# A decoder kernel's first attention stages: stack units and cross slots moved, batch 0's cross mask added in PSUM

## The reference

```python
x = x + _L0_attn_ref(_layernorm(x), Wq, Wk, Wv, Wo, lambda_q1, ...)      # differential, 8 heads x 2
x = x + _L0_xattn_ref(ctx, ctx, _layernorm(x), mask, W_fc, b_fc)          # 16 heads of 8

def _L0_xattn_ref(value, key, query, mask, W_fc, b_fc):
    energy = jnp.einsum('nqhd,nkhd->nhqk', q, k)
    energy = jnp.where(mask == 0, -1e20, energy)
    attention = jax.nn.softmax(energy / jnp.sqrt(E), axis=3)
    out = jnp.einsum('nhql,nlhd->nqhd', attention, v).reshape(N, Sq, E)
    return out @ W_fc.T + b_fc
```

## Time and profile before

| what | us |
|---|---|
| median of 3 runs | 1274.69 |
| lowest, highest | 1274.1, 1276.63 |
| profiled execution | 1273.83 |
| its span | 1272.5 |
| PE, DVE, ACT, POOL busy | 1040.1, 812.6, 610.1, 232.6 |

### The profile page before, as it was taken

The page is one execution under the profiler, slowest core; times in us unless marked ns, Lnnn a source line. Parts: engine busy times, 40 slices in busy tenths (PEclk is TensorE's granted clock), DMA queues, the critical chain, the costliest instruction groups (busy, mean ns, idle before and its releaser), DMA issues.

```text
span 1272.5 us, 19904 instructions
## 1 busy us (share of the span) xinstructions
PE 1040.1 (82%) x7649; PEld 557.8 (44%) x7649; DVE 812.6 (64%) x2015; ACT 610.1 (48%) x1015; POOL 232.6 (18%) x299
## 2 busy tenths in 40 slices
PE   6777689998999965677675889999647978769999
PEld 4233223333677652344542333566412333346757
DVE  7787867722115468878776881677688886565422
ACT  2456356564334428768652677323115556323342
POOL 2933300000000223765621000001210000010000
PEclk9789779997899985766876999999857888779999
DMA  8342140000000300346014202600100300000000
GB/s 299 91 87 67 41 160 2 2 2 1 1 1 1 100 34 1 105 122 125 1 44 136 100 2 35 106 1 1 50 23 11 119 1 2 33 1 1 1 9 9
DMA packets 34785, 61.29 MB, mean 48 GB/s; under 512 B 4771, under 2 KB 25076, under 8 KB 33092
## 3 DMA queue, kind: packets, MB, share of 16 engines
q1 hardware_dynamic: 33828, 58.70, 16.5%
q10 hardware_dynamic: 864, 1.33, 0.3%
HBM read 42.98 MB, written 16.65 MB: 47 GB/s over the span
## 4 chain that ended last, share of the span: by engine, by line
PE 59%; DVE 29%; ACT 4%; issue 4%; DMA 2%; POOL 1%; SPq 0%; DVEq 0%; ACTq 0%; POOLq 0%
PE ps_s L851 9%; PE ps_e L841 9%; PE ps_v L644 6%; DVE mx L1798 6%; PE ps_e L580 5%; PE ps_e L578 3%; PE ps_s L601 3%; PE ps_e L938 2%; PE ps_s L925 2%; DVE ps_s L1794 2%; DVE mx L1788 2%; DVE work L2274 2%; ACT work L1346 2%; DVE work L2276 2%; DVE xn L1754 1%
## 5 line engine op out<-in xcount | busy, mean ns | idle before, releaser
L1346 ACT ACTIVATE work<-ps_e 128x512 f32<-128x512 f32 x448 | 250.6, 598 | 149.4 <-PE ps_e L580 144.1
L2546 POOL TENSOR_TENSOR rstd<-rstd,halves 128x2 f32<-128x2 f32 x52 | 36.6, 704 | 752.8 <-DVE rstd L1741 752.7
L1798 DVE TENSOR_REDUCE mx<-ps_s 128x2 f32<-128x1024 f32 x128 | 153.9, 1222 | 28.8 <-PE ps_s L601 27.3
L601 PE MATMUL ps_s<-ctx_stack,q_stack 49*128 49x512 bf16 (+1 forms) x384 | 128.3, 452 | 50.0 <-DVE mx L1798 36.5
L1448 ACT ACTIVATE work<-ps_s,keep 128x512 f32<-128x512 f32 x136 | 93.0, 687 | 145.5 <-PE ps_s L851 142.5
L580 PE MATMUL ps_e<-q_stack,ctx_stack 52*128 52x256 bf16 (+1 forms) x768 | 150.9, 297 | 12.3 <-DMA q_stack<-mT 5.0
L644 PE MATMUL ps_v<-work,vaug 128*32 128x256 f32 x1536 | 133.2, 424 | 4.6 <-ACT work L1334 4.6
L841 PEld LDWEIGHTS ps_e<-ffn_w,work 128*128 128x128 f32 x960 | 119.3, 198 | 21.0 <-issue 19.9
L851 PE MATMUL ps_s<-xnT,ffn_w 128*128 128x512 f32 x240 | 119.7, 627 | 3.6 <-ACT work L1448 3.6
L841 PE MATMUL ps_e<-ffn_w,work 128*128 128x128 f32 x960 | 121.3, 282 | 0.8 <-DVE x L1990 0.8
L2000 DVE SCALAR_TENSOR_TENSOR x<-ps_e,gates,x 128x128 f32<-128x128 f32 x128 | 39.0, 347 | 127.0 <-PE ps_e L841 123.9
(11 more groups left out here) (373 smaller groups left out, 1812.1 us busy)
## 6 DMA issues: line engine op xcount, KB each, us to landing
q_stack<-q_scr SPq DMA_DIRECT2D x32, 192.0 KB
ffn_w<-in_L0f_w SPq DMA_DIRECT2D x1, 4608.0 KB, 14.7
ffn_w<-in_L1f_w SPq DMA_DIRECT2D x1, 3456.0 KB, 13.0
q_scr<-parts SPq DMA_DIRECT2D x16, 192.0 KB, 2.1
c_scr<-ffn_w SPq DMA_DIRECT2D x12, 256.0 KB, 7.6
kx_scr<-ffn_w SPq DMA_DIRECT2D x12, 256.0 KB, 3.5
ctx_stack<-kx_scr SPq DMA_DIRECT2D x2, 1536.0 KB
ctx_stack<-c_scr SPq DMA_DIRECT2D x2, 1536.0 KB
```

What stands on the lines that cost most here:

```text
L601: return pe.matmul(ps_s[i][:, parity, :], q_stack[p0:p0 + n_rows, b, pair, part * P:(part + 1) * P], ctx_stack[p0:p0 + n_rows, pair, b * S ...
L1346: act.activation(pt[:, parity, :, :].rearrange("p k q -> p (k q)"), bank[f"e{parity}"], ACT.Exp).then_inc(exped, 1)
L1798: m = dve.tensor_reduce(mx[:, b, :, pair, part], ps_s[i][:], AX, ALU.max, negate=True)
```

## The change

`OVERLAP` goes from 36 to 32. The queries' units of batch 1 leave the prologue for slots 0 to 3, its keys' units go from 0 to 3 to slots 4 to 7. The context units of batch 0 go from slots 3 to 10, one each, to slots 8 to 11, two each. Batch 0's x units go from 33, 34, 34, 35 to 30, 30, 31, 31; batch 1's from 41, 42, 42, 43 to 38, 38, 39, 39. The mask transposes go from 37, 38, 39, 45 to 33, 34, 36, 37. The norm for the cross stage is transposed and copied one slot earlier. In batch 0 each cross score bank is first filled with the mask by an identity matmul, and the score matmul adds to it; DVE then takes one plain negated reduction over both banks, and the sign change of L1807 is left out. PE waits for the two mask tiles of batch 0 before the first cross step. Batches 1 to 3 stay with the custom operation.

```diff
-OVERLAP = 36
+OVERLAP = 32
-STACK_FIRST = stack_units("q", 0), stack_units("k", 0) + stack_units("q", 1)
-MASK_AT = [37, 38, 39, 45]
+STACK_FIRST = stack_units("q", 0), stack_units("k", 0)
+MASK_AT = [33, 34, 36, 37]
 STACK_AT = {}
-for units, slots in ((stack_units("k", 1), range(4)), (stack_units("c", 0), range(3, 11)),
-                     (stack_units("x", 0), (33, 34, 34, 35)), (stack_units("x", 1), (41, 42, 42, 43)),
+for units, slots in ((stack_units("q", 1) + stack_units("k", 1), range(8)),
+                     (stack_units("c", 0), (8, 8, 9, 9, 10, 10, 11, 11)),
+                     (stack_units("x", 0), (30, 30, 31, 31)), (stack_units("x", 1), (38, 38, 39, 39)),
                      (stack_units("c", 1), (44, 44, 45, 45, 46, 46, 47, 47))):
...
             pair, part = h // 2 % 8, h % 2
+            masked = use == X0 and b == 0
+            if masked:
+                pe.matmul(ps_s[i][:, parity, :], ident_b[:], far_q[:, part, :], start=True, stop=False,
+                          skip_group_check=True)
             return pe.matmul(ps_s[i][:, parity, :], q_stack[p0:p0 + n_rows, b, pair, part * P:(part + 1) * P],
-                             ctx_stack[p0:p0 + n_rows, pair, b * S2:(b + 1) * S2], start=True, stop=True)
+                             ctx_stack[p0:p0 + n_rows, pair, b * S2:(b + 1) * S2], start=not masked, stop=True,
+                             skip_group_check=masked)
...
-                if at == 7:
+                if at == 6:
                     turn_norm("L0x", b)
...
+            if t == 0 and use == X0:
+                pe.wait_ge(far_done, TPB)
...
-                if at == 8:
+                if at == 7:
                     turned_norm("L0x", b, qT, scale=RSQRT128)
...
-                if use == X0:
+                if use == X0 and b > 0:
                     for parity in range(2):
                         m = dve.tensor_tensor_reduce(ps_s[i][:, parity, :], ps_s[i][:, parity, :],
...
-            if use == X0:
+            if use == X0 and b > 0:
                 settle(dve.tensor_scalar(col, col, -1.0, None, ALU.mult))
```

## The result

The changed kernel is slower by 0.7%: median 1281.55 us of 20 runs (1272.24 to 1293.13) against 1272.17 us of 20 runs of the kernel before (1263.6 to 1279.8). The ratio is 1.0072, 95% interval [1.0045, 1.0099], which is +9.2 us (5.7 to 12.6) where +11.2 was forecast. The profiled execution took 1276.23 us (span 1274.9), 5 us less than that median.

The account below looks back on a forecast made before the run. Latency before 172.2 us, then PE, bounds the kernel; only the shift of the first cross exponents counts. Terms -1.0 + 0 + 1.0 + 12.2 - 1.5 + 0.5 = +11.2 us, plus 0.86 on 1273.83: 1286 us, 8-in-10 range 1272.5 to 1292.

Parts of the forecast that it names:

- The tie: First cross exponents wait, through SP's fixed order, for batch 3's queries: 11.66 us after batch 3's norm transpose.
- E0: First exponent matmul of the cross stage, slot 56; at 162.21 us before, forecast at 173.4; its shift is the time change.
- Masks, +12.2: Batch 0's cross score steps: 13 masked steps on PE's path, each +0.94 us, together +12.2 us.
- lower end of 8.4: Mask term with no extra at the change from 128 rows to 56: a step grows by 0.65, 8.4 us.
- DVE, -1.5: Batch 0's cross maxima: plain reductions shorten DVE's work, counting only where PE waits for it; -1.5 us (0 to -2.9).
- Three more score steps, +1.0: Before batch 3's norm transpose: 19 score steps instead of 16, 0.33 us each, +1.0 us.
- units moved, 0: Batch 0's cross units, from slots 33 to 35 to 30 and 31, and batch 1's units: 0 (batch 0's ends -1, +1).
- Prologue, -1.0: Batch 1's query units leave the prologue, context units double up in slots 8 to 11: -1.0 us (-2.3 to 0).
- Split in slot 47, +0.5: DVE's split of batch 0's maxima falls between batch 3's close and its add: +0.5 us (0 to +2.5).
- After E0, unchanged: Stretch behind the first cross exponents keeps its length, 140 us to the mixture, with the same slots and closings left.
- Rival C: Slower: idle PE before E0 keeps the clock at 1.2 GHz longer, masked steps not hidden; +16.5 us, 1291, chance 0.11.
- Rival A: Faster: DVE and four earlier slots decide, PE's gaps take the masks whole; 5.2 us off, 1269.5, chance 0.14.

Follow-up runs that it names:

- moves only: The changed kernel without mask matmuls and the far_done wait, custom maximum for all batches, all slots moved; ratio 0.9983 to the kernel before.
- paired masks: The changed kernel with both mask matmuls ahead of both scores in each masked step; ratio 1.0024 to the kernel before.
- x4: The changed kernel with SP writing batch 0's maxima row ahead of batch 3's queries; ratio 1.0002 to the kernel before.
- x5: The changed kernel without mask matmuls, SP writing batch 0's maxima row ahead of batch 3's queries; ratio 0.9908 to the kernel before, median 1261.75 us.
- Masks only: The kernel before with batch 0's cross mask laid into PSUM by identity matmul and nothing moved; ratio 1.0032, median 1278.62 us.
- x11: The kernel before with batch 0's row placed after the write of batch 3's queries and ahead of their fill; ratio 0.9978, median 1269.54 us.
- x6: The kernel before with only SP's order changed, batch 0's row ahead of batch 3's queries; ratio 0.9962.
- x7: The kernel before with only the early query, key and context units moved as in the change; ratio 0.9988.
- x10: The kernel before with the early units moved and SP's order changed, cross slots still from 36; ratio 0.9968.
- x1: The kernel before with batch 0's cross mask laid into PSUM by identity matmul and nothing moved; ratio 1.0032.

## Why the prediction was right, point by point

The mechanism was right: the tie to batch 3's queries and the masks on PE's way. That the sum came so close (+11.2 for +9.2) is in part luck. Two terms that were put at nothing, the moved slots and the clock, were off by 3 to 4 us each, in opposite directions; the estimates stand in the last section.

**The tie.** "E0 is the transpose of batch 3's norm plus 11.66 us" held: 11.7 before, 12.0 in the changed kernel, 11.5 in moves only and 11.6 in paired masks, and 2.5 in x4 and x5, where SP's order was changed. This was the step on which the whole forecast rested, and x4 shows it.

**Masks, +12.2.** A step of mask, score, mask, score measured 1.28 us against 0.33: +0.95, forecast +0.94. The ratios put the masks with DVE's relief at 0.9% (changed against moves only) and 0.9% again (x4 against x5), some 11 to 12 us; the forecast had 12.2 - 1.5 = 10.7. Masks only (nine steps) came out lower, at 0.3%. The lower end of 8.4, a mask beside which nothing is lost at the change of row counts, is out: the score piece also took 0.32. The Trainium skill, page TensorEngine Tiling (Array Packing), section Key Properties under Tiling Modes, says that changing the tiling mode drains TensorE. It gives no size. The trace agrees with it: a step with two changes (paired) takes 0.86 us, one with four 1.28, some 0.2 us for each change that goes. But the paired order also lets the two scores run beside each other, and no run here separates the two.

**DVE, -1.5.** The waits for DVE's maxima on PE's way fell from 4.9 to 3.6 us in the changed kernel, and to 2.2 in masks only, while DVE's own wait for PE rose from 2.0 to 9.3. A relief that is small and mostly unusable, as forecast; its size was not isolated.

**Three more score steps, +1.0, and units moved, 0.** Moves only has a ratio of 0.9983, the forecast of its parts was -1.0 + 1.0 = 0. Right within its interval, some 2.9 us either way. But the profiles say otherwise. The last group's transpose is at 141.1 us in moves only and at 141.2 in x5, and at 137.4, 137.9 and 140.1 in the three kernels with the old slots and no masks (before, x11, x6). That is 1 to 4 us later where 0 was forecast. The ratio doesn't show it because this kernel's executions had a higher granted clock; at equal clock the moves cost about 3.4 us by the estimate at the end. Which of the moved pieces costs them was not tested.

**Prologue, -1.0.** Slot 12 came 2.7 us earlier in the changed kernel (53.02) and 2.1 in x7 than in the one profile of the earlier trace rows (55.74). But that profile is the latest of the four with the old prologue (54.8 to 55.7, mean 55.1); the eight with the new one have 53.0 to 54.5, mean 53.7. The gain is 1.4 us, near the forecast. The forecast had three extra units, one in slot 10 and two in 11, at half clock, 0.98 us each. PE's timeline of the changed kernel shows that part of that was not paid in it:

```profile
49.85 1.07 PE L676 MATMUL ps_e<-ffn_w 128*32 128x512 bf16 x6
50.85 0.40 PE L597 MATMUL ps_s<-self_stack,q_stack 56*128 56x256 bf16 x4
51.18 0.39 PE L696 MATMUL ps_e<-ffn_w 128*32 128x512 bf16 x2
51.19 0.61 PE L676 MATMUL ps_e<-ffn_w 128*32 128x512 bf16 x6
...
53.02 0.28 PE L581 MATMUL ps_e<-q_stack,self_stack 56*128 56x256 bf16 x1 [0.77 <-DMA q_stack<-mT]
```

The last unit of slot 10 takes 1.07 us, at half clock; from 50.85 the clock is full again, and the first of slot 11 takes 0.61. The first maximum of DVE starts at 32.72 (36.03 in the earlier trace rows, 33.7 forecast). In the whole time x7 has 0.1%, not told from 0.

**Split in slot 47, +0.5.** It took 0.85 us of DVE (153.79 to 154.64) in the changed kernel, but from the last group's transpose to the norm's transpose it was 13.2 us in both (137.37 to 150.55, 146.27 to 159.44): 0. It lies behind POOL's root (149.05 to 151.96), between DVE's close at 152.19 and its add at 155.92. The three masked steps of slots 45 to 47, also put at 0, lie in the same 13.2 us.

**After E0, unchanged.** 147.8 us to the mixture's first up-projection before, 145.9 after: 1.9 us less. (The prediction's 140 us reach only to the stage's end near 303.) The clock came back 5.7 us after E0 instead of 10.1. So E0 moved by 9.2 us in the two profiles and the mixture by 7.3. Rival C put a longer half clock on the idle stretch. In this profile it is shorter; in those of moves only and of paired masks, with nearly the same idle ahead of E0, it is longer, 14.1 and 14.5 us. So the profiles do not settle rival C. Over all executions the changed kernel spent less time at half clock, not more, and this is the term that was missed; its size is estimated at the end.

The forecast's own range was added up to +19.9 us at its upper end; its terms give +19.5. Nothing hangs on it.

Rival A had 5.2 us off and the gaps taking the masks whole. The gaps for ACT stayed: 3.0 us of waits for its lift in both kernels; the masks pushed them along.

## What to carry to other kernels

Before work is put earlier, find what its consumer waits for: here four slots of earlier scores fed a row whose write stood behind another batch's DMAs in SP's list, and by themselves they bought nothing that can be told from no change (moves 0.9983, order 0.9962, both 0.9908; how much of the last is the clock's stands at the end). Moving work between engines pays only if the receiver has slack on the same stretch: the masks freed a DVE that PE had waited for 4.9 us, and lengthened PE's way so that DVE waited 9.3 us for its scores. Where matmuls of 128 rows and of row pairs must mix, put those of a kind next to each other; that alone took 0.42 us off each step's 0.95. And where the granted clock differs between kernels, a ratio holds two things, the path and the clock; look at both before a small difference is put down to the edit.

## What the runs showed of the hardware that was not expected

**The clock's return after E0.** All twelve kernels come to E0 at 1.2 GHz, and the time until 2.4 GHz is granted differs: 10.1 us after E0 before, 5.7 in the changed kernel, 14.1 and 14.5 in moves only and paired masks, 3.6 in x6, whose windows are

```profile
164.10:167.70 3.60, 3.60 (x13) 0.75 (x13) 1.53 (x6) 1.48 (x3) 0.00 (x0) 0.50 0.38 101
167.70:177.00 9.30, 9.11 (x69) 2.75 (x68) 7.82 (x24) 6.88 (x12) 0.00 (x0) 1.00 1.01 391
```

In the table, the stretch from E0 to the mixture goes with its time at half clock: 147.8 to 149.2 us with 18.1 to 19.5 at half (seven kernels), 145.9 and 146.0 with 12.8, 145.2 with 8.6 or 8.7 (x6, x10, x11). That is about 0.3 us for each us at half clock.

**The clock in all executions.** Each row of this table rests on all recorded executions and not on one profile. The record has the mean granted clock of each; as the twelve traces hold no level but 1.2 and 2.4 GHz, it gives the time spent at half clock. Over 209 executions, each compared with the mean of its own kernel, the time rises by 0.24 us for each us at half clock (correlation 0.88), and most of the scatter of single executions goes with it. The last column takes that share out. It is an estimate, good to 1 to 2 us, and it assumes that the same 0.24 holds between kernels. All differences are in us, of means, to the kernel before in the same set of runs (mean clock 0.862 to 0.864); the changed kernel is put beside the set that was run with x1 to x4.

| kernel | mean granted clock | time at half clock | time | time at equal clock |
|---|---|---|---|---|
| changed | 0.870 | -17.6 | +9.4 | +13.7 |
| masks only | 0.868 | -13.8 | +6.1 | +9.4 |
| moves only | 0.869 | -16.4 | -0.5 | +3.4 |
| changed, masks paired | 0.869 | -16.9 | +3.1 | +7.2 |
| changed, SP reordered | 0.873 | -26.0 | +0.1 | +6.4 |
| moves only, SP reordered | 0.875 | -32.9 | -11.5 | -3.6 |
| before, SP reordered | 0.867 | -12.6 | -5.0 | -1.9 |
| before, prologue of the change | 0.864 | -3.8 | -1.9 | -1.0 |
| paired, SP reordered | 0.875 | -31.9 | -10.2 | -2.5 |
| prologue, SP reordered | 0.868 | -11.5 | -4.8 | -2.0 |
| before, row between write and fill | 0.866 | -6.5 | -3.4 | -1.8 |

Read so, the masks with DVE's relief cost 10.3 and 10.0 us (changed less moves only, x4 less x5; 10.7 forecast), the prologue gives 1.0 (1.0 forecast), the moves cost 3.4 (0 forecast), and SP's order gives 7 to 10 us in the kernels with slots from 32 and 1.9 in the kernel before. Some 3 of the 4.8 us that x6 gains go with its clock, and some 8 of the 11.5 of x5. At equal clock x5 is 1.7 us below x6 and 1.6 below x10, which this estimate can't tell from nothing: that the moves pay once the order is changed rests on the ratios. Why these kernels are granted the full clock for longer is not shown by any run.

**The row behind the fill.** From the issue of batch 0's row to E0 it took 3.8 to 4.3 us in the six kernels where the row stands right behind the fill of `q_stack` for batch 3 (3.9 before: 158.28 to 162.21), and 3.1 to 3.2 in the six where it stands ahead of it. x11 changes only the fill's place and has 3.2.

**Row groups.** Two 56-row matmuls at partitions 0 and 64 into different banks took 0.32 us together to the next 128-row matmul, and a single one between 128-row matmuls took 0.32 as well.
